# An attention layer by distances, then experts: a feature stage of 16 operations and eight turned groups

## What is computed

```python
x = x + _L0_attn_ref(_layernorm(x), ...)
    V = (x @ wv.T + bv)                      # 16 heads of 16
    pos = x @ w3d.T + b3d                    # a point of 3 coordinates for each row
    dist = _pairwise_l2(pos)                 # sqrt of the sum of squares
    attn = softmax(causal(-dist / 4))        # the same for all heads
    out = (attn @ V) @ wo.T + bo
x = x + _L0_ffn_ref(_layernorm(x), ...)      # 8 experts, top 2, and 2 shared ones
```

## Time and profile before

| | before |
|---|---|
| median of 3 runs | 620.65 us (618.48 to 622.29) |
| profiled execution | 619.65 us, its span 617.9 us |
| TensorE matmuls, share of the span | 552.0 us, 89% |
| VectorE | 439.9 us, 71% |
| ScalarE | 329.2 us, 53% |
| GpSimd | 270.7 us, 44% |

### The profile page before, as it was taken

The page is one execution under the profiler, slowest core; times in us unless marked ns, Lnnn a source line. Parts: engine busy times, 40 slices in busy tenths (PEclk is TensorE's granted clock), DMA queues, the critical chain, the costliest instruction groups (busy, mean ns, idle before and its releaser), DMA issues.

```text
span 617.9 us, 11503 instructions
## 1 busy us (share of the span) xinstructions
PE 552.0 (89%) x3468; PEld 480.7 (78%) x3468; DVE 439.9 (71%) x1218; ACT 329.2 (53%) x684; POOL 270.7 (44%) x577
## 2 busy tenths in 40 slices
PE   4879899996989969819999998999999999999984
PEld 3865799986589966518888887888888888887874
DVE  7858998583997746696777654666666666665696
ACT  3447998264998706504545432455555555555321
POOL 4038500125740016006666661477777776776000
PEclk9879899997989998967999999899999999999999
DMA  8999000000000019102222222233333333331895
GB/s 258 323 328 27 1 1 2 2 1 1 1 2 1 1 40 396 76 0 96 88 88 83 93 87 62 70 106 104 106 108 108 106 104 105 106 104 65 274 355 200
DMA packets 57129, 63.03 MB, mean 102 GB/s; under 512 B 14736, under 2 KB 50448, under 8 KB 57072
## 3 DMA queue, kind: packets, MB, share of 16 engines
q1 hardware_dynamic: 49216, 43.75, 25.0%
q0 software_dynamic: 6480, 17.90, 8.2%
q10 hardware_dynamic: 1376, 0.66, 0.4%
HBM read 30.64 MB, written 31.65 MB: 101 GB/s over the span
## 4 chain that ended last, share of the span: by engine, by line
PE 55%; DVE 6%; issue 1%; ACT 1%; POOL 0%; DVEq 0%; POOLq 0%
PE bank L1322 16%; PE bank L1323 15%; PE bank L1324 15%; PE bank L1445 3%; PE bank L1461 2%; PE bank L1330 1%; PE bank L1374 1%; DVE YG L1223 1%; DVE h_lo L1252 0%; DVE X L1233 0%; PE bank L1347 0%; DVE mv L1083 0%; DVE hf L1242 0%; DVE X L1215 0%; DVE XN L1086 0%
## 5 line engine op out<-in xcount | busy, mean ns | idle before, releaser
L974 POOL DMA_INDIRECT token_out<-YS,to_row x71 | 71.7, 1010 | 49.2 <-DVE back L1289 45.2
L938 POOL DMA_INDIRECT slots_in<-X,slot x64 | 66.1, 1033 | 60.3 <-DVE slot L1199 30.5
L676 PE MATMUL a_bank<-VO,E_hi 128*128 128x258 f32 x272 | 78.5, 289 | 3.5 <-issue 1.8
L680 PE MATMUL a_bank<-VO,E_lo 128*128 128x258 f32 x272 | 78.5, 289 | 0.0
L678 PE MATMUL a_bank<-VO,E_hi 128*128 128x256 f32 x272 | 78.2, 287 | 0.0
L1278 DVE TENSOR_TENSOR hr<-bank,sr 128x256 f32<-128x256 f32 x71 | 30.1, 425 | 60.1 <-ACT sr L1045 60.1
L1322 PE MATMUL bank<-W_hi,XST_hi 128*128 x142 | 62.4, 440 | 0.5 <-DVE XST_lo L1294 0.5
L1045 ACT ACTIVATE sr<-bank 128x256 f32<-128x256 f32 x71 | 27.2, 383 | 63.9 <-PE bank L1324 63.9
L1323 PE MATMUL bank<-W_lo,XST_hi 128*128 x142 | 56.8, 400 | 0.0
L1019 ACT ACTIVATE h_hi<-hf 128x512 fp32r<-128x512 f32 x32 | 20.2, 632 | 68.6 <-DVE hf L1242 68.6
L1324 PE MATMUL bank<-W_hi,XST_lo 128*128 x142 | 56.3, 397 | 0.0
(11 more groups left out here) (247 smaller groups left out, 1657.6 us busy)
## 6 DMA issues: line engine op xcount, KB each, us to landing
XS<-slots_in SPq DMA_DIRECT2D x71, 131.0 KB, 2.0
slots_in<-blank SPq DMA_DIRECT2D x7, 1179.0 KB, 15.5
YG<-token_out SPq DMA_DIRECT2D x16, 512.0 KB, 8.8
W_raw<-in_wT_dram SPq DMA_DIRECT2D x8, 768.0 KB, 13.2
X<-in_x_dram SPq DMA_DIRECT2D x8, 512.0 KB, 8.1
out_dram<-X SPq DMA_DIRECT2D x32, 128.0 KB, 2.8
token_out<-YS,to_row POOLq DMA_INDIRECT x71, 2.5
slots_in<-blank SPq DMA_DIRECT2D x1, 1048.0 KB, 13.8
```

The costliest lines, as they stand in the source:

```text
L676: pe.matmul(O_ps[Q % 2][j][:, 0:D + 2], E_hi[:, n % NE, cols], VO[:, kt, 0:D + 2], start=(kt == 0), stop=False)
L680: mm = pe.matmul(O_ps[Q % 2][j][:, 0:D + 2], E_lo[:, n % NE, cols], VO[:, kt, 0:D + 2], start=False, stop=(kt == qt))
L938: pool.indirect_dma_start(out=xs, out_offset=bass.IndirectOffsetOnAxis(ap=slot[k][:, t:t + 1], axis=0), in_=X[:, t, :], in_offset=None).th ...
L974: pool.indirect_dma_start(out=ys, out_offset=bass.IndirectOffsetOnAxis(ap=to_row[:, i:i + 1], axis=0), in_=YS[:, i % NYS, :], in_offset=No ...
```

## The change

- The grid comes from a bound of the coordinates, not from their maximum: the largest sum over w3d squared (reach, two small matmuls and a square root by ScalarE, before the values) plus the largest of b3d. VectorE turns it into the magic number after the second group of values of batch 0 (five small operations, scale_of_positions), once for both batches.
- Features are 16 VectorE operations (N_POS counts 15 on s_f, and one of them is the copy of the two norms into FK) and five of ScalarE (key_terms and two more, counted on s_fka), which fill two tables, FQ and FK. FK holds both halves of the key's terms in 128 rows; ScalarE copies a turned group of it twice, scaled by a column of part that is 1 for 32 rows and 0 for the others, into KTh and KTl.
- Eight groups are turned, through banks 4 to 7. Three (Q0, K0, Q1) come before the squares, the others after blocks of the first half; VectorE copies groups 0 and 2, ScalarE the others, five of them among its square roots. The squares wait for the group that they need (copied).
- Between the last values and the features TensorE transposes the identity 44 times into a bank that nobody reads.
- c_ps is made in the head, before the values, from bv_all that ScalarE writes first; ScalarE copies it to shift, GpSimd adds bo. add_shift waits for the statistics (s_st) and the turned x (s_T) and comes ahead of all diagonals.

```diff
-N_FQ, N_FKH, N_POS = 30, 34, 45
+N_H, N_LH, N_LL, N_FQ, N_POS = 2, 4, 7, 14, 15
+N_ACT, N_DVE = 10, 2
+N_IDLE = 44
...
+        TURNS = [("Q", 0), ("K", 0), ("Q", 1), ("K", 1), ("Q", 2), ("Q", 3), ("K", 2), ("K", 3)]
+        N_FIRST = 3
+        BY_DVE = (0, 2)
... GpSimd
-                for F in (FQ, FKh, FKl):
-                    pool.memset(F[:, :, :], 0.0).then_inc(s_fz, 1)
+                for F, at in ((FQ, ONE_Q), (FK, ONE_K)):
+                    pool.memset(F[:, :, :, :], 0.0).then_inc(s_fz, 1)
+                    pool.wait_ge(s_fz, 4 * b + (2 if F is FQ else 4) - 1)
+                    pool.memset(F[:, :, 0:2, at:at + 2], 1.0).then_inc(s_fz, 1)
...
-                pool.wait_ge(s_f, N_POS * (b + 1))
-                pool.wait_ge(s_shift, 1)
-                add_shift(range(TB - GT))
+                if b == 0:
+                    pool.wait_ge(s_c, 1)
+                    pool.wait_ge(s_bo, 16)
+                    pool.tensor_tensor(shift[:, :], shift[:, :], bo_all[:, :], ALU.add).then_inc(s_shift, 1)
+                    pool.wait_ge(s_shift, 1)
+                pool.wait_ge(s_st, TB * (b + 1))
+                for g in range(GB):
+                    pool.wait_ge(s_T, KC * ((b * GB + g) + 1))
+                    add_shift(range(g * GT, g * GT + GT))
                 for kt in range(half):
                     diagonal(kt)
-                add_shift(range(TB - GT, TB))
... ScalarE
+                if b == 0:
+                    act.wait_ge(s_bcol, 16)
+                    for c in range(KC):
+                        act.activation(bv_all[:, c, :], ...)
                 group_hi(0)
                 if b == 0:
                     deviation(0, 1)
                     ...
+                    act.wait_ge(s_cps, 1)
+                    act.activation(shift[:, :], c_ps, ACT.Copy).then_inc(s_c, 1)
+                    act.wait_ge(s_rps, 1)
+                    act.activation(reach[:, :], reach_ps, ACT.Sqrt, scale=float(D * D)).then_inc(s_reach, 1)
...
+                act.activation(FK[:, :, 0, 0:3], terms[:, :, 0:3], ACT.Copy, scale=-2.0).then_inc(s_fka, 1)
+                act.activation(FQ[:, :, 0, 0:3], terms[:, :, 0:3], ACT.Copy).then_inc(s_fka, 1)
+                key_terms(3, 2, 0)
+                act.wait_ge(s_f, N_POS * b + N_LH)
+                key_terms(9, 3, 3)
+                act.wait_ge(s_f, N_POS * b + N_LL)
+                key_terms(18, 3, 6)
...
+                def turn_out(n):
+                    kind, g = TURNS[n]
+                    act.wait_ge(s_ft, len(TURNS) * b + n + 1)
+                    if kind == "Q":
+                        act.activation(QT[0:NR, columns(g)], F_ps[n % 4][0:NR, :], ACT.Copy).then_inc(s_fr, 1)
+                    else:
+                        act.activation(KTh[...], F_ps[n % 4][0:NR, :], ACT.Copy, scale=part[0:NR, 0:1])...
+                        act.activation(KTl[...], F_ps[n % 4][0:NR, :], ACT.Copy, scale=part[0:NR, 1:2])...
+                for n in range(N_FIRST):
+                    if n not in BY_DVE:
+                        turn_out(n)
...
                     for kt in range(GT * half[-1] + GT):
                         row = row_of(half, kt)
+                        if rows == 0 and N_FIRST + kt < len(TURNS):
+                            turn_out(N_FIRST + kt)
... VectorE, the features
+                put(dve.tensor_scalar(hsum[:, :, :], pos[:, :, :], magic[:, 0:1], None, ALU.add))
+                after(1)
+                put(dve.tensor_scalar(h, hsum[:, :, :], magic[:, 0:1], None, ALU.subtract))
+                after(2)
+                put(dve.tensor_tensor(l[:, :, :], pos[:, :, :], h, ALU.subtract))
+                after(3)
+                put(dve.tensor_copy(lh.bitcast(f32r), l[:, :, :]))
+                put(dve.tensor_tensor(t3[:, :, :], h, h, ALU.mult))
+                put(dve.scalar_tensor_tensor(out=t3b[:, :, :], in0=h, scalar=2.0, in1=l[:, :, :], ...))
+                after(4)
+                put(dve.tensor_tensor(ll, l[:, :, :], lh, ALU.subtract))
+                after(5)
+                put(dve.tensor_reduce(nrm[:, :, 0], t3[:, :, :], AX.X, ALU.add))
+                after(6)
+                put(dve.tensor_tensor(t3b[:, :, :], t3b[:, :, :], l[:, :, :], ALU.mult))
+                after(9)
+                put(dve.tensor_reduce(nrm[:, :, 1], t3b[:, :, :], AX.X, ALU.add))
+                dve.wait_ge(s_fz, 4 * (b + 1))
+                after(7)
+                put(dve.tensor_copy(FQ[:, :, 1, 0:27].rearrange("p t (a c) -> p t a c", a=3),
+                                    terms[:, :, :].unsqueeze(2).to_broadcast([P, TB, 3, 9])))
+                after(10)
+                put(dve.tensor_copy(nrm2[:, :, :, 0].bitcast(f32r), nrm[:, :, :]))
+                after(12)
+                put(dve.tensor_tensor(nrm2[:, :, :, 1], nrm[:, :, :], nrm2[:, :, :, 0], ALU.subtract))
+                after(13)
+                put(dve.tensor_copy(FQ[:, :, 0:2, ONE_K:ONE_K + 2], nrm2[:, :, :, :]))
+                put(dve.tensor_copy(FK[:, :, 0:2, ONE_Q:ONE_Q + 2], nrm2[:, :, :, :]))
+                for n in BY_DVE:
+                    dve.wait_ge(s_ft, len(TURNS) * b + n + 1)
+                    dve.tensor_copy(QT[0:NR, columns(TURNS[n][1])], F_ps[n % 4][0:NR, :]).then_inc(s_frd, 1)
... TensorE
+            pe.wait_ge(s_bv, KC)
+            for cd in range(KC):
+                mm = pe.matmul(c_ps, bv_all[:, cd, :], woT_raw[:, cd, :], start=(cd == 0), stop=(cd == KC - 1))
...
+                def turn(n):
+                    kind, g = TURNS[n]
+                    pe.wait_ge(s_f, N_POS * b + (N_FQ if kind == "Q" else N_POS))
+                    pe.wait_ge(s_fka, 5 * b + 5)
+                    if n >= 4:
+                        copied(n - 3)
+                    F = FQ if kind == "Q" else FK
+                    for j in range(GT):
+                        mm = pe.transpose(F_ps[n % 4][0:NR, j * P:(j + 1) * P], F[:, g * GT + j, :, :]..., ident[:, :])
+                    mm.then_inc(s_ft, 1)
+
+                for j in range(N_IDLE):
+                    pe.transpose(F_ps[3][:, (j % GT) * P:(j % GT + 1) * P], ident[:, :], ident[:, :])
+                for n in range(N_FIRST):
+                    turn(n)
+                first = len(halves[0])
+                need = {(0, 0): 2, (1, 0): 3, (1, GT): 4, (2, 0): 6, (2, 2 * GT): 7, (3, 3 * GT): 8}
                 for n, (Q, kt) in enumerate(sq_blocks):
+                    if (Q, kt) in need:
+                        copied(need[Q, kt])
...
+                    if Q == first - 1 and N_FIRST + kt < len(TURNS):
+                        turn(N_FIRST + kt)
```

More of the change, by code:

```diff
@@ L90, in attention_and_experts @@
         shift = sb("shift", [P, D])
-        one_f = sb("one_f", [1, P])
+        w3_sq = sb("w3_sq", [P, KC, 3])
+        reach = sb("reach", [P, 3])
+        most = sb("most", [P, 2])
+        part = sb("part", [P, 2])
         ident = sb("ident", [P, P])
@@ L177, in attention_and_experts @@
         s_f = sem("s_f")
-        s_pt = sem("s_pt")
+        s_c = sem("s_c")
+        s_w3q = sem("s_w3q")
+        s_rps = sem("s_rps")
+        s_reach = sem("s_reach")
+        s_part = sem("s_part")
+        s_magic = sem("s_magic")
+        s_fka = sem("s_fka")
         s_ft = sem("s_ft")
         s_fr = sem("s_fr")
+        s_frd = sem("s_frd")
         s_q = sem("s_q")
@@ L216, in attention_and_experts, with copied_by_act, copied_by_dve, columns @@
         NROW = sum(GT * half[-1] + GT for half in halves)
+        TURNS = [("Q", 0), ("K", 0), ("Q", 1), ("K", 1), ("Q", 2), ("Q", 3), ("K", 2), ("K", 3)]
+        N_FIRST = 3
+        BY_DVE = (0, 2)
+        def copied_by_act(n):
+            return sum(2 if TURNS[m][0] == "K" else 1 for m in range(n) if m not in BY_DVE)
+        def copied_by_dve(n):
+            return sum(m in BY_DVE for m in range(n))
+        def columns(g):
+            return slice(g * GT * P, (g + 1) * GT * P)
         def row_of(half, kt):
@@ L243, in _ @@
             pool.memset(ident[:, :], 0.0).then_inc(s_const, 1)
-            pool.memset(one_f[:, :], 1.0).then_inc(s_const, 1)
+            pool.memset(part[:, :], 0.0).then_inc(s_const, 1)
             pool.memset(eps_col[:, :], EPS).then_inc(s_const, 1)
@@ L457, in _ @@
                                                  op1=ALU.subtract).then_inc(s_vol, 1)
+                    if b == 0 and g == 1:
+                        scale_of_positions()
                 step = [0]
@@ L595, in values @@
                     pe.wait_ge(s_vol, GT * G + j + 1)
+                    if G == 0 and j == 2:
+                        pe.wait_ge(s_c, 1)
+                    if G == 0 and j == 3:
+                        pe.wait_ge(s_reach, 1)
                     tok = slice(j * P, (j + 1) * P)
@@ L622, in _ @@
                         if g == 0:
+                            pe.wait_ge(s_w3q, 1)
+                            for c in range(KC):
+                                mm = pe.matmul(reach_ps, mean_of[:, :], w3_sq[:, c, :],
```

(12 more changed lines are left out.)

154 lines of the change are left out of this document (63 added, 91 removed).

## The result

| | before | after |
|---|---|---|
| median of the runs | 620.62 us (618.48 to 622.29) | 612.85 us (611.66 to 614.5) |
| profiled execution | 619.65 us, span 617.9 us | 611.66 us, span 609.9 us |

The ratio is 0.9857, 95% interval 0.9821 to 0.9893: 1.4% faster. The time lies 1.05 us above the forecast of 611.8 and inside its range.

The account below looks back on a forecast made before the run. The feature stage, a chain through one engine at a time with no engine near full, was taken to delay all that follows. Gains of 3.2 and 7.1 us, less 0.7 twice, make 8.9 us: 611.8 us, range 607.8 to 615.5.

Parts of the forecast that it names:

- The operations before the turns: Feature stage, small operations between the last values and the first turn: 3.0 us instead of 5.3.
- The identity turns: Feature stage: 44 transposes take 4.7 us, hold the clock through a 1.2 us gap; 1.7 us paid in batch 1.
- Rival B: Feature stage: the clock falls under the identity turns too, about 2.1 us lost in batch 1, 613.9 us; chance 0.15.
- The collision: Feature stage, batch 0: GpSimd's additions hold the chain's first operation until 38.0; features ready at 41.0, 2.2 us after identity turns.
- D: Values: GpSimd's additions also block operations with one PSUM and one SBUF operand, 15.5 us lost, 624.0 us; chance 0.03.
- rival A: Feature stage, batch 0: no collision, small operations slip between the additions; start 3.3 us earlier, 608.5 us; chance 0.24.
- Behind that gap of 2.2 us the clock has most likely fallen: Batch 0, between identity turns and features: slower turns and first squares cost 1.2 us, between 0 and 2.
- Eight groups, three first: First real turn to first product of the squares: 2.25 us instead of 8.27 and 8.87.
- The five groups inside the squares: First half of the squares: the thirteenth block comes about 0.7 us late in each batch, 0.3 to 1.0.
- ScalarE's copies, costed at nothing: Squares into weighted sum: eight copies delay exponentials 2.2 us, but slack of 2.2 us remains, 0.5 if clock holds.
- The head: Before the values: ScalarE starts 2.4 us later waiting for bv_col; net between -0.5 and +2.4 us, taken as 0.
- rival C: Head: ScalarE's wait of 2.4 us is not won back, 614.2 us; chance 0.12.

Follow-up runs that it names:

- both controls: The changed kernel run again without edits, on other chips: 614.39 us, ratio 0.9867, and 617.74 us, ratio 0.9884, to the kernel before.
- the three edits together: Changed kernel with 22 identity turns instead of 44, GpSimd's additions released group by group, ScalarE's bv_col wait behind its first two x copies: 605.01 us, ratio 0.9722.

## Why the prediction was right, and which steps were not

- *What bounds.* Right: 12.35 us left the feature stages and 9.0 arrived at the border; the other 3.3 are the longer stretches of the table above, the values and twice the squares.
- *The operations before the turns*, 3.0 us. In batch 1 they took 2.8 us from the first one's start (135.08 to 137.87); with the collision 5.5. Right.
- *The identity turns*, 4.7 us, holding the clock through a gap of 1.2 us: they took 5.02 with the tail, the clock was 1.00 under them, the gap 1.22. In batch 1 2.2 us were paid instead of 1.7, as features were ready sooner. Rival B did not happen. (The gap at 28 that the prediction leaned on begins there and ends at 29.8; that the clock stayed up through it is so.)
- *The collision.* That GpSimd blocks operations that read SBUF alone, and not the one with a PSUM operand, was right (D fell by L547 at 0.47 us). Its size was not. The additions reached 4.0 us into the chain, as forecast (3.9: to 38.0 from 34.1; measured to 39.43 from 35.43). But features were ready 5.4 us after VO, not the 6.9 of the forecast (41.0 against 34.1): the step "the chain's first operation waits for the additions, until 38.0" failed. It ran at once, and the operations behind it went through one for each addition, which was the reason of rival A. So the gap behind the identity turns was 0.36 us and not 2.2, and VO to SQ, 7.95 us, lies nearer to A's (6.97) than to the forecast (10.3). The two executions with the held operation did go by the row of L412. The Trainium skill's rule (SBUF — State Buffer, "SBUF: two separate sides"), a lock for one whole instruction, gives one operation of VectorE for each addition; the trace agrees in that, with 0.58 to 0.76 us an operation beside additions of 0.64, and does not in the two executions with 2.57 and 2.60 us, four additions long. Nor does it agree that GpSimd is blocked in its turn: the additions lost nothing. The estimate of 40.9 by that rule came 1.4 us late too, about what six waits of GpSimd for 0.2 us each would add.
- *Behind that gap of 2.2 us the clock has most likely fallen*, 1.2 us. This term failed with the gap: the clock stayed at 1.00. Its price was right where the fall was made to happen, 0.84 us. Together the collision (1.5) and this term (1.2) were sized 2.7 us too high in batch 0.
- *Eight groups, three first*, 2.25 us from turn to SQ: 2.51 and 2.45. Right to 0.3; ScalarE's copies of a K group last 0.69 us, not 0.6.
- *The five groups inside the squares*, 0.7 us in each batch, 0.3 to 1.0: 1.07, just outside. TensorE's 6.6 us were right; I had priced the thirteenth block only, and VectorE has lost it all by its ninth evacuation. "The 40 evacuations within 21.5 us" missed as well, with 21.88.
- *ScalarE's copies, costed at nothing.* No wait at block 12 that the border shows.
- *The head, "I take 0".* This step failed: +1.35 us, rival C in part. By the prediction's own sign (wrong "if the values stage grows by more than 1 us") the forecast was wrong here, though its time came out. The bound of +2.4 held in this pair of executions; in others the values were longer still. I had named the table load and not counted it; it made the start 3.7 us later instead of 2.4.
- *The sum.* 8.9 forecast, 9.01 measured. By stretch the measured differences lie +1.35 (head), -2.4 (features of batch 0, the 2.7 less 0.3 of the turns), +0.25 and +0.35 (squares) and +0.3 (features of batch 1) from the forecast ones. That the total is so near is luck: in batch 0 most of rival A happened, and part of rival C paid for it. What bounds, the 3.0 us of the chain, the turns and batch 1 are not luck. The 145.4 named for the first product of batch 1 is in the time of the kernel before; with the gain of batch 0 taken off it is 142.9, and 142.53 was measured.

## What to carry to other kernels

Work that only holds the clock has to be sized by the wait that it fills: enough to reach the moment the real work is ready, not more, since it stands ahead of it in the queue. Such filling, or any other slack, hides what lies beside it; an edit that shortens it shows collisions and waits that had cost nothing, so try the two together. And when work is moved into the head of a kernel, count what each engine's queue waits for in front of its first useful instruction, a load and a table load included.

## What the runs showed of the hardware

- Small VectorE operations that read SBUF (128x48) ran at 0.58 to 0.76 us beside GpSimd's additions of 0.64 us, instead of 0.2, and the additions lost nothing (16 in 10.30 us); in two of nine executions one was held for 2.57 and 2.60 us, to the end of the additions. The cast L412, 5.24 us across three memsets before, took 1.75 us in the changed kernel, where GpSimd waits on a semaphore behind its first large memset and makes a small one: it went on when that first memset ended.

```profile
2.24 1.80 POOL L290 MEMSET FQ<- 128x2048 f32 x1
2.33 1.75 DVE L486 CAST VO<-one_zero 128x32 fp32r<-128x32 f32 x1 [2.33 <-POOL ident L284]
4.10 0.20 POOL L292 MEMSET FQ<- 128x64 f32 x1
4.19 1.82 POOL L290 MEMSET FK<- 128x2048 f32 x1
```

- In the kernel without identity turns the clock fell behind an idle time of 3.83 us only after TensorE had been back at work for 0.6 us (batch 1), but 2.2 us into one of 6.16 us (batch 0). Gaps of 1.22 and 1.62 us in the feature stages brought no fall, while in the kernel before the clock fell behind one of 1.3 us at 36. One and the same gap of 1.75 us, ahead of the sum of batch 0, was followed by a fall in the changed kernel and both controls, and by none with 22 identity turns and with the three edits together. Length of the gap alone did not decide it.
- The unchanged second part took between 388.1 and 396.5 us in profiled executions, more than most of the edits were worth.
